# Delta-rule layer of a decoder: products inside a chunk of 32 tokens as 32x32 blocks on four diagonal tiles instead of padded 64x64 blocks on two

## The reference, cut to what matters

```
A  = strictly lower part of (beta * k) @ k.T        # 32 x 32 within the chunk
T  = inverse of (I + A)                             # unit lower triangular
u  = T @ (beta * v)
w  = T @ (beta * k)
for each chunk i:  u_i = u[i] - w[i] @ S
                   o_i = q[i] @ S + (q[i] @ k[i].T, lower part) @ u_i
                   S   = S + k[i].T @ u_i
```

## Time and profile before

| | |
|---|---|
| median of 3 runs | 1435.24 us (1424.43 to 1436.36) |
| span of the profiled execution | 1418.5 us |
| PE busy / PEld busy | 1334.8 / 1166.4 us |
| DVE busy | 991.1 us |
| ACT busy | 682.2 us |
| product batches L2210, PE busy | 103.1 us in 3072 records |
| filter taps L2337, PE busy | 108.6 us in 2624 records |

### The profile page before, as it was taken

How to read it: one execution, slowest core, us unless ns; L and a number is a source line. 1 busy time by engine, 2 the same in 40 slices (tenths; PEclk the granted TensorE clock), 3 DMA queues, 4 the chain that set the end, 5 groups by cost and what they waited for, 6 DMA issues and landing times.

```text
span 1418.5 us, 42978 instructions
## 1 busy us (share of the span) xinstructions
PE 1334.8 (94%) x18644; PEld 1166.4 (82%) x18644; DVE 991.1 (70%) x2959; ACT 682.2 (48%) x1735; POOL 137.9 (10%) x299
## 2 busy tenths in 40 slices
PE   6999998999986899999999999999999999999997
PEld 6788887888643689899789889788979879989976
DVE  7957898678689554667784567796457778455767
ACT  3535763448377456333447533346632444743332
POOL 3111121111110010100110100011010010010000
PEclk9989999999997899999999999999999999999999
DMA  5000000000230200000000000000000000000001
GB/s 160 2 3 2 3 2 2 3 2 3 77 139 19 77 2 1 2 3 2 2 2 1 2 3 3 1 2 1 1 2 4 2 3 1 1 1 3 3 2 31
DMA packets 8509, 20.33 MB, mean 14 GB/s; under 512 B 2304, under 2 KB 6400, under 8 KB 7808
## 3 DMA queue, kind: packets, MB, share of 16 engines
q1 hardware_dynamic: 8320, 17.58, 3.5%
HBM read 16.53 MB, written 1.05 MB: 12 GB/s over the span
## 4 chain that ended last, share of the span: by engine, by line
PE 47%; DVE 12%; ACT 4%; issue 2%; POOL 1%; DVEq 0%
PE PS L2210 6%; PE PS L2337 6%; PE PS L1935 4%; PE PS L1967 3%; PE PS L1956 3%; PE PS L1922 3%; PE PS L2220 3%; PE PS L589 2%; PE PS L690 2%; ACT AR L1985 2%; PE PS L1947 2%; PE PS L2669 1%; PE PS L2678 1%; PE PS L1819 1%; DVE X L2740 1%
## 5 line engine op out<-in xcount | busy, mean ns | idle before, releaser
L589 PE MATMUL PS<-CC 128*128 128x128 f32 x1024 | 134.9, 279 | 0.0
L589 PEld LDWEIGHTS PS<-CC 128*128 128x128 f32 x1024 | 124.5, 193 | 3.1 <-issue 0.5
L1985 ACT ACTIVATE AR<-PS,SC 128x128 f32<-128x128 f32 x256 | 91.1, 378 | 39.3 <-DVE SC L2013 39.3
L2337 PE MATMUL PS<-AR,PA 64*64 64x256 f32 (+43 forms) x2624 | 108.6, 300 | 0.5 <-issue 0.4
L2210 PEld LDWEIGHTS PS<-AR 64*64 64x64 f32 x3072 | 100.5, 135 | 7.2 <-issue 2.2
L2210 PE MATMUL PS<-AR 64*64 64x32 f32 (+1 forms) x3072 | 103.1, 219 | 0.8 <-DVE AR L2463 0.3
L576 POOL TENSOR_SCALAR SC<-mv 128x2 f32<-128x2 f32 x64 | 13.2, 206 | 837.0 <-DVE mv L562 818.4
L2337 PEld LDWEIGHTS PS<-AR,PA 64*64 64x64 f32 x2624 | 85.0, 133 | 6.9 <-issue 2.7
L2010 DVE TENSOR_REDUCE SC<-PS 128x4 f32<-128x512 f32 x64 | 44.2, 691 | 57.1 <-PE PS L1935 56.7
L1935 PE MATMUL PS<-kvt,AR 128*128 128x128 f32 x512 | 68.8, 279 | 2.6 <-ACT AR L1980 2.6
L1935 PEld LDWEIGHTS PS<-kvt,AR 128*128 128x128 f32 x512 | 63.2, 191 | 7.9 <-ACT AR L1980 6.6
(11 more groups left out here) (552 smaller groups left out, 3334.6 us busy)
## 6 DMA issues: line engine op xcount, KB each, us to landing
WC<-in_cw SPq DMA_DIRECT2D x1, 5438.5 KB, 15.8
PA<-in_fd SPq DMA_DIRECT2D x1, 2624.0 KB, 9.3
PA<-in_stat SPq DMA_DIRECT2D x2, 1280.0 KB, 12.0
X<-in_x SPq DMA_DIRECT2D x2, 512.0 KB, 5.5
out<-X SPq DMA_DIRECT2D x1, 1024.0 KB, 5.3
CC<-in_const SPq DMA_DIRECT2D x1, 809.0 KB, 4.4
PA<-in_aw SPq DMA_DIRECT2D x1, 653.0 KB, 7.4
PA<-in_intw SPq DMA_DIRECT2D x1, 576.0 KB, 5.8
```

Source lines behind the costliest of these rows:

```text
L589: T.matmul(bank[int(b)][:, 0:P], lhsT=ident, rhs=CC[:, 0:P], start=True, stop=True)
L1985: A.activation(d.blocks[:, h, :], d.bank[:, h * P:(h + 1) * P], ACT.Exp, scale=D2 ** -0.5, bias=d.most[:, h:h + 1], accum_out=d.total[:, h ...
L2337: m = T.matmul(out_[:, :, first:SEQ], lhsT=FD[rows, tap:tap + 64], rhs=d.vp[rows, :, first + 1 - shift:SEQ + 1 - shift], start=starts, sto ...
```

## The change

The 10 batches of a unit that stay inside a chunk (`up`, `step`, `y`, `w`) go through a new function `chunk_products`: 8 blocks by 4 quarters of the partitions, 32 matmuls, each with a weight block of 32x32, quarter b of the partitions to quarter b of the output. The two batches that join the chunks (`z`, `delta`) stay in `products`. The padded copies are gone: ACT's `ttw`, the 64-wide `pcw` and its gate copy `ddw` on DVE. The two 512-wide DVE operations of the fourth round are 256 wide. Waits on ACT's copy become waits on DVE's transpose, and DVE's transpose waits for no copy any more. The tables of turns are the same.

```diff
--- before.py
+++ after.py
@@ -2176,14 +2176,13 @@
                 self.gram, self.lt = pairs(3584), pairs(4096)
                 self.fir = [ar[:, o:o + 512] for o in (3584, 4608)]
                 self.up = [pairs(4608 + 512 * n) for n in range(5)]
-                self.acc, self.pcw = ar[:, 5120:5632], pairs(5120)
+                self.acc = ar[:, 5120:5632]
                 self.g32 = pairs(7168)
-                self.tc, self.tt, self.ttw = chunks(7680), chunks(7936), pairs(8192)
+                self.tc, self.tt = chunks(7680), chunks(7936)
                 self.zv = self.tc
                 self.xtp = st.kvt[:, :, 0:SEQ + 3]
                 self.beta, self.dd, self.br = (sc[:, o:o + 8].rearrange("p (h j) -> p h j", j=TS) for o in (8, 48, 56))
                 self.ss, self.rr = (sc[:, o:o + 16].rearrange("p (k h j) -> p k h j", k=2, j=TS) for o in (16, 32))
-                self.ddw = sc[:, 608:624].rearrange("p (n g) -> p n g", g=2)
                 self.grams = ps[:, 0:2, :].rearrange("p b (f n) -> p (b f) n", f=4)
                 self.bank = {b: ps[:, b, 0:256].rearrange("p (n k) -> p n k", k=32) for b in (2, 3)}
                 self.pr, self.p4 = ar[:, 3072:4352], ar[:, 1536:2816].rearrange("p (n d) -> p n d", d=32)
@@ -2204,12 +2203,22 @@
         def tensor_l3_attention(st):
             k, ps, sc, d = "L3a", st.ps, st.sc, Delta(st)
             p, a, v = st.pe, st.act, st.dve
-            def products(name, bank, lhs, rhs, width=32):
+            def products(name, bank, lhs, rhs):
                 for n in range(8):
                     for rows in d.halves:
-                        m = T.matmul(ps[rows, bank, n * width:(n + 1) * width], lhsT=lhs[rows, n, :], rhs=rhs(rows, n),
+                        m = T.matmul(ps[rows, bank, n * 32:(n + 1) * 32], lhsT=lhs[rows, n, :], rhs=rhs(rows, n),
                                      start=True, stop=True)
                 m.then_inc(*p.up(name))
+
+            def chunk_products(name, bank, lhs, rhs):
+                for n in range(8):
+                    for b, rows in enumerate(d.quarters):
+                        m = T.matmul(ps[rows, bank, n * 32:(n + 1) * 32], lhsT=lhs(rows, b, n), rhs=rhs(rows, n),
+                                     start=True, stop=True)
+                m.then_inc(*p.up(name))
+
+            def turned(rows, b, n):
+                return d.tt[rows, n, :]
 
             yield from tensor_norm(st, k)
             T.wait_ge(*a.at(f"{k}.xt"))
@@ -2256,25 +2265,26 @@
             for n in range(1, 5):
                 T.wait_ge(*v.at(f"{k}.mask{n}"))
                 T.wait_ge(*v.at(f"{k}.inverse{n - 1}"))
-                products(f"{k}.up{n}", 2, d.up[n], lambda rows, n: d.tc[rows, n, :])
+                chunk_products(f"{k}.up{n}", 2, lambda rows, b, i: d.up[n][rows, i, 32 * (b % 2):32 * (b % 2) + 32],
+                               lambda rows, i: d.tc[rows, i, :])
                 yield
                 T.wait_ge(*v.at(f"{k}.scaled{n}"))
-                T.wait_ge(*a.at(f"{k}.wide{n - 1}"))
+                T.wait_ge(*v.at(f"{k}.turned{n - 1}"))
                 if n < 4:
-                    products(f"{k}.step{n}", 3, d.ttw, lambda rows, n: d.pc[rows, n, :])
+                    chunk_products(f"{k}.step{n}", 3, turned, lambda rows, n: d.pc[rows, n, :])
                 else:
-                    products(f"{k}.step{n}", 3, d.pcw, lambda rows, n: d.ttw[rows, n, :], width=64)
+                    chunk_products(f"{k}.step{n}", 3, lambda rows, b, n: d.pc[rows, n, :], lambda rows, n: d.tt[rows, n, :])
                 yield
             T.wait_ge(*v.at(f"{k}.inverse4"))
             T.wait_ge(*v.at(f"{k}.bv"))
-            products(f"{k}.y", 2, d.ttw, lambda rows, n: d.bv[rows, n % TS, 32 * (n // TS):32 * (n // TS) + 32])
+            chunk_products(f"{k}.y", 2, turned, lambda rows, n: d.bv[rows, n % TS, 32 * (n // TS):32 * (n // TS) + 32])
             yield
             T.wait_ge(*v.at(f"{k}.across"))
             T.wait_ge(*v.at(f"{k}.y"))
             products(f"{k}.z", 3, d.g32, lambda rows, n: d.yv[rows, n, :])
             yield
             T.wait_ge(*v.at(f"{k}.z"))
-            products(f"{k}.w", 2, d.ttw, lambda rows, n: d.zv[rows, n, :])
+            chunk_products(f"{k}.w", 2, turned, lambda rows, n: d.zv[rows, n, :])
             yield
             T.wait_ge(*v.at(f"{k}.w"))
             T.wait_ge(*v.at(f"{k}.lt"))
@@ -2425,10 +2435,6 @@
             A.copy(d.lt, d.grams[:, :, 0:64]).then_inc(*a.up(f"{k}.local"))
             yield
             for n in range(4):
-                A.wait_ge(*v.at(f"{k}.turned{n}"))
-                for c in range(2):
-                    A.activation(d.ttw[:, :, 32 * c:32 * c + 32], d.tt, ACT.Copy, scale=cc("halves")[:, c:c + 1]).then_inc(
-                        *a.up(f"{k}.wide{n}" if c else None))
                 yield
             A.wait_ge(*p.at(f"{k}.fir"))
             A.wait_ge(*v.at(f"{k}.path_delta"))
@@ -2484,8 +2490,6 @@
             V.tensor_tensor(sc[:, 48:56], sc[:, 48:56], sc[:, 8:16], ALU.mult).then_inc(*v.up())
             V.tensor_tensor(sc[:, 56:64], sc[:, 40:48], sc[:, 8:16], ALU.mult).then_inc(*v.up())
             yield
-            V.wait_ge(*v.now())
-            V.tensor_tensor(d.ddw, bc(sc[:, 48:56], 2, 2), bc(cc("halves"), 1, 8), ALU.mult).then_inc(*v.up())
             yield
             mask(0, "low1")
             yield
@@ -2521,11 +2525,7 @@
             late = slice(4, 5)
             for n in range(1, 5):
                 V.wait_ge(*p.at(f"{k}.up{n}"))
-                if n < 4:
-                    V.tensor_tensor(d.pc, d.bank[2], dd8, ALU.mult).then_inc(*v.up(f"{k}.scaled{n}"))
-                else:
-                    V.tensor_tensor(d.pcw.rearrange("p n (g k) -> p n g k", g=2), bc(d.bank[2], 2, 2), bc(d.ddw, 3, 32),
-                                    ALU.mult).then_inc(*v.up(f"{k}.scaled{n}"))
+                V.tensor_tensor(d.pc, d.bank[2], dd8, ALU.mult).then_inc(*v.up(f"{k}.scaled{n}"))
                 if n < 4:
                     mask(n + 1, f"up{2 ** (n + 1)}")
                 yield
@@ -2534,7 +2534,6 @@
                     V.tensor_tensor(d.tc, d.tc, d.bank[3], ALU.subtract).then_inc(*v.up(f"{k}.inverse{n}"))
                     yield
                     V.wait_ge(*v.now())
-                    V.wait_ge(*a.at(f"{k}.wide{n - 1}"))
                     V.transpose(d.tt, d.tc).then_inc(*v.up(f"{k}.turned{n}"))
                     if n == 1:
                         yield
@@ -2543,8 +2542,7 @@
                     elif n == 2:
                         V.tensor_tensor(d.g32, d.gram, bc(cc("across"), 1, 8), ALU.mult).then_inc(*v.up(f"{k}.across"))
                 else:
-                    V.tensor_tensor(d.ttw, d.ttw, ps[:, 3, :].rearrange("p (n k) -> p n k", k=64),
-                                    ALU.subtract).then_inc(*v.up(f"{k}.inverse4"))
+                    V.tensor_tensor(d.tt, d.tt, d.bank[3], ALU.subtract).then_inc(*v.up(f"{k}.inverse4"))
                 yield
             V.wait_ge(*p.at(f"{k}.y"))
             V.tensor_copy(d.yv, d.bank[2]).then_inc(*v.up(f"{k}.y"))
```

## The result

The changed kernel is slower: 1468.6 us (median of 4 runs, 1461.65 to 1478.39) against 1429.84 us (4 runs, 1422.27 to 1436.36) for the kernel before on the same chip. The ratio is 1.029, 95% interval 1.022 to 1.036. The prediction was 1418 us with a range up to 1446: wrong in sign, and outside the range.

A forecast was written before the change was run, and what follows sets the result against it. The prediction took TensorE, working through its list nearly without a stop, to bound the kernel. Batches -33.8, switches +14.9, DVE -0.5 and new waits +2 made -17.4 us, from 1435.24 to 1418 us; range 1404 to 1446.

The forecast's parts named there:

- The first term: In 80 product batches, 64 passes on four tiles replace 32 on two: 0.42 us less each, -33.8 us.
- The first rival: Inside each 32x32 batch, instructions come too slowly; at 14 ns a pass +14 us, 1449 us; chance 0.16.
- Switches: On TensorE between block shapes: 93 new switches at 0.16 us each, +14.9 us.
- ACT: ACT loses 64 copies, 29.0 us of its time; taken as no gain, at best 1 us.
- DVE's waits: Dependent batches wait more for DVE's results: +2 us, bounds 0 and 8.
- narrower operations: DVE's shorter fourth round saves 5.6 us of its time; 0.5 us where TensorE waits for it.
- The clock: Rival: in the delta rule the clock halves for stretches, 28 us lost, +11 us, 1446 us; chance 0.05.
- DVE takes over: Rival: DVE, 83% busy in one stretch, brings 8 us of waits, 1424 us, or 1429; chance 0.15.
- The sum: Whole kernel: -33.8 + 14.9 - 0.5 + 2 = -17.4 us.
- The floor under each matmul: Rival: in the batches every pass costs 25 ns however small, +70 us, 1506 us; chance 0.03.

The follow-up runs named there:

- half: The changed kernel with half of the blocks of each 32x32 batch left out, so 32 passes a batch: ratio 0.987 to the kernel before.
- copies: The changed kernel with ACT's 64 copies put back, read by nobody: ratio 1.041 to the kernel before.
- step32: The changed kernel with the four up batches of each unit back in 64x64 blocks, 48 batches in 32x32: ratio 1.020 to the kernel before.
- splittaps: The kernel before with taps of shift 1 to 28 that neither open nor close a filter split into two matmuls: ratio 1.012 to the kernel before.
- switch: The kernel before with one small 32x32 matmul ahead of each of the 80 batches: ratio 1.019 to the kernel before.
- up32: The kernel before with only the four up batches of each unit (32 batches) in 32x32 blocks: ratio 1.011 to the kernel before.
- hybrid: The kernel before with 32x32 blocks only in 25 batches chosen for few or no new shape switches: ratio 1.000 to the kernel before.
- wide: The changed kernel with every 32x32 pass moving its 32 columns twice: ratio 1.029 to the kernel before.
- burst64: The kernel before with 512 extra 64x64 passes on two tiles, then 512 on four, ahead of one step batch: second part 12.6 us; no ratio.
- the two bursts: burst64, and the kernel before with one up batch's product repeated ahead of it (512 32x32 passes, 256 64x64, 512 moving 64 columns): first part 12 us; no ratios.

## Why the prediction was wrong, point by point

**The first term's pace: right for a batch, wrong for a stretch.** The prediction took 7.9 ns a pass "since the 14 ns are explained by the tiles themselves (58/4) and nothing in those rows waits for instructions". The trace shows 8.9 ns in the first batch and 8.5 ns over 190 passes, so the array side held: 80 x (0.93 - 64 x 0.0085) = 31 us. The step that failed is the one behind it: that a pace seen for some passes lasts. With 38 to 50 us of stops the first term was +7 to +19 us, where the prediction had -33.8. The earlier trace rows show 28 passes; a block has 128, and blocks fetched ahead cover a short run of small passes. Its sentence was true of its rows and no evidence. The same goes for the 29 ns of the product batches, which it explained by 58/2 alone, while 14.6 ns an instruction gives 29.2 too. Nothing in a trace in which both limits agree can tell which one holds; the count of instructions per stretch could have warned. One batch and 24 taps were 112 instructions in 2.05 us, 18 ns each; the forecast made that 176 in 1.95 us, 11 ns each. At 13.9 to 14.6 ns they take 2.45 to 2.57 us.

**The first rival: right mechanism, wrong size.** "Instructions don't come fast enough" had 0.16. Its price came from a batch alone, at 14 ns a pass, so at most 2.4 us of gain were left and the end was +14. But the supply is 14 ns an *instruction*, 28 a pass, and it is shared with the taps: their spare time is used up too. The stops cost 38.4 us by the matmuls' idle time, 54.6 - 4.9 = 50 by the loads' idle time for issue (L2216, L2209, L2347, less L2210 and L2337 before).

**Switches.** 0.16 us each and 93 of them; measured 0.11 to 0.14 us and 93. 10 to 13 us in place of 14.9.

**ACT.** 0 in full-speed time by the run with the copies put back. **DVE's waits.** +2 us was taken. Loads and matmuls together, on all batches, waited 3.9 us for DVE before and 7.5 after: +4. Its narrower operations show (985.8 against 991.1 us busy), and win nothing.

**The clock.** Its rival had 0.05 and a price of 28 us; 14 us came on average, 10 in the profiled execution. Drains and narrow work, its cause, are not borne out: half has as many switches and hardly a stop, and its clock loss is that of the kernel before (39.7 us). Nor are the stops. From 590 to 1400 us the clock was low for 27 us in the changed kernel, copies and step32, for 17 in half, switch and splittaps, for 10 in up32, for 7 in before and hybrid, and for 3 in wide, each in one execution: wide has 26 us of stops and the least, splittaps and switch have hardly any and more than up32. In burst64 three stops of 0.6 to 1.7 us passed at a granted clock of 1.00. What brings the clock down stays open, and with the spread of the runs so does how much of its loss the change made.

**DVE takes over** is out for the changed kernel (6.5 us of waits) but is what limits half.

**The sum** in full-speed time: -31 for the array, +10 to +13 for switches, +4 for DVE, +38 to +50 for stops make +21 to +36; measured +29. With 14 us for the clock that is the 43 us between the mean spans. The stops are taken from the same trace that they explain, so the sum shows that nothing large is missing, no more.

**The floor under each matmul** is out: 8.5 ns between passes on four tiles, 34 ns on a tile. The Trainium skill, TensorE: Matmul & The Clock Gate, section Back-to-back issue gap, gives some 25 ns as the floor for 1 to 64 moved columns; the traces agree only if that is counted within one tile.

## What to carry to other kernels

Count instructions, not only array time. Where a change trades few large matmuls for many small ones, divide the time of the whole stretch (small work and what lies beside it) by its instructions, TensorE's weight loads included, and compare with the shortest time for an instruction that the kernel has kept up so far over several hundred of them; here 14 to 15 ns was the end, and the kernel before stood on it inside each batch. A rate seen over fewer instructions than one fetched block shows what the array can do, not what it will be fed. And where runs swing by more than the effect, multiply the span by its mean granted clock: that number had a standard deviation of 1.8 us where the span alone had 5.6.

## What the runs showed of the hardware

- TensorE's instructions come in blocks of 16 KB, 256 instructions. Where it waits for them, one block comes every 3.3 to 3.8 us, at a granted clock of 0.50 and of 1.00 alike: 13.6 to 14.6 ns an instruction in the two bursts. The Trainium skill, Advanced Engine Details and Errata, section ISA Cache, states cache lines of 16 KB, 256 instructions each, and only two of them, beside a size of 128 KB on TensorE. The traces agree with the 256, and with two lines rather than with 128 KB in that no more than 380 small instructions ran ahead of a stop.
- A fetch is not bound by bytes: in 600 to 660 us the 15 blocks took 1.6% of 16 engines' time, 1.0 us each, on queues with next to nothing else on them. What sets the 3.7 us was not tried.
- Fetching ahead covered 190 passes (380 instructions) at 8.5 ns in one burst, and 133 in the other, which came behind 512 passes at the limit.
